# A graph network's counting groups with ten slots in two sets, their bounds loaded ahead, and the heads' additions on VectorE

## The reference, cut to what matters

```python
# first attention level, H = 8 heads, C = 768
h = (x @ W).reshape(n, H, C)
alpha_s = jnp.einsum('nhc,hc->nh', h, a_s)
alpha_d = jnp.einsum('nhc,hc->nh', h, a_d)
e = jax.nn.leaky_relu(alpha_s[src] + alpha_d[dst], NEG_SLOPE)
m = jax.ops.segment_max(e, dst, num_segments=n)
e = jnp.exp(e - m[dst])
denom = jax.ops.segment_sum(e, dst, num_segments=n)
alpha = e / (denom[dst] + EPS)
out = jax.ops.segment_sum(h[src] * alpha[:, :, None], dst, num_segments=n) + b
h = jax.nn.elu(out)          # and h @ W2 goes into the second level
```

## Time and profile before

| what | us |
|---|---|
| runs | 1856.82, 1858.04, 1856.78, median 1856.82 |
| the profiled execution, its own time | 1852.02 |
| its span, first to last instruction | 1849.9 |
| PE busy, mean granted clock | 1708.2, 0.971 |
| PE weight loads | 1387.4 |
| DVE busy | 1283.4 |
| ACT busy | 772.0 |
| POOL busy | 558.3 |

### The profile page before, as it was taken

How to read it: one execution, slowest core, us unless ns; L and a number is a source line. 1 busy time by engine, 2 the same in 40 slices (tenths; PEclk the granted TensorE clock), 3 DMA queues, 4 the chain that set the end, 5 groups by cost and what they waited for, 6 DMA issues and landing times. The chain is left out here.

```text
span 1849.9 us, 22198 instructions
## 1 busy us (share of the span) xinstructions
PE 1708.2 (92%) x7573; PEld 1387.4 (75%) x7582; DVE 1283.4 (69%) x2168; ACT 772.0 (42%) x1276; POOL 558.3 (30%) x319
## 2 busy tenths in 40 slices
PE   3779999999989999999999899999999994989998
PEld 1248888878867878777778777788787872878898
DVE  6654445544588877888789778887888428984437
ACT  4213332222345554455345545554455324534240
POOL 0012312212234533354335334434354213320003
PEclk9989999999999999999999999999999996989999
DMA  3015565495564546455555644566454412132123
GB/s 129 1 55 173 188 220 195 160 232 189 171 235 129 191 157 151 133 200 171 177 117 190 196 121 141 188 169 164 126 195 160 156 54 78 52 115 77 52 70 118
DMA packets 133808, 268.02 MB, mean 145 GB/s; under 512 B 23739, under 2 KB 83525, under 8 KB 121029
## 3 DMA queue, kind: packets, MB, share of 16 engines
q1 hardware_dynamic: 133700, 266.63, 45.6%
HBM read 206.21 MB, written 60.40 MB: 144 GB/s over the span
## 5 line engine op out<-in xcount | busy, mean ns | idle before, releaser
L466 POOL TENSOR_TENSOR w2l<-w2r,w2h 128x768 fp32r<-128x768 f32 x96 | 210.7, 2195 | 353.6 <-ACT w2h L587 353.6
L41 PE MATMUL bank<-ph,hc 128*128 128x512 f32 x768 | 300.9, 392 | 11.4 <-DVE mean L877 10.2
L42 PE MATMUL bank<-pl,hc 128*128 128x512 f32 x768 | 300.2, 391 | 0.0
L43 PE MATMUL bank<-ph,hc 128*128 128x512 f32 x768 | 300.1, 391 | 0.0
L753 DVE CUSTOM_DVE_ANT_0 junk<-bank,a_bc 128x512 bf16<-128x512 f32 (+1 forms) x256 | 129.9, 554 | 192.7 <-ACT st L527 176.8
L41 PE MATMUL bank<-hh,w2h 128*128 128x512 f32 x576 | 230.7, 400 | 21.8 <-DVE hl L886 18.3
L462 POOL TENSOR_TENSOR psum_rows<-psum_rows,pf 128x512 f32<-128x512 f32 x96 | 165.8, 1727 | 213.1 <-DVE pf L811 213.1
L41 PE MATMUL bank<-wh,xTh 128*128 128x512 f32 x570 | 224.0, 393 | 5.4 <-POOL wl L452 5.4
L43 PE MATMUL bank<-hh,w2l 128*128 128x512 f32 x576 | 226.5, 393 | 0.0
L42 PE MATMUL bank<-hl,w2h 128*128 128x512 f32 x576 | 226.1, 392 | 0.0
L42 PE MATMUL bank<-wl,xTh 128*128 128x512 f32 x570 | 222.6, 391 | 0.0
(11 more groups left out here) (245 smaller groups left out, 3081.3 us busy)
## 6 DMA issues: line engine op xcount, KB each, us to landing
hc<-h_scratch SPq DMA_DIRECT2D x96, 1024.0 KB, 4.9
h_scratch<-st SPq DMA_DIRECT2D x96, 512.0 KB, 3.0
w2r<-in_L_gnn_W SPq DMA_DIRECT2D x96, 384.0 KB, 4.9
wr<-in_L_gnn_W SPq DMA_DIRECT2D x12, 1536.0 KB, 8.5
gwr<-in_L_gnn_W SPq DMA_DIRECT2D x24, 384.0 KB, 3.3
row_bc<-logits_scratch SPq DMA_DIRECT2D x16, 512.0 KB, 10.5
expo_bc<-expo_scratch SPq DMA_DIRECT2D x16, 512.0 KB, 5.8
xr<-in_x SPq DMA_DIRECT2D x2, 1536.0 KB, 8.2
```

The lines of the kernel that those rows point to most:

```text
L41: nc.tensor.matmul(out, sh, mh, start=first, stop=False, skip_group_check=not grouped)
L42: nc.tensor.matmul(out, sh, ml, start=False, stop=False, skip_group_check=not grouped)
L43: return nc.tensor.matmul(out, sl, mh, start=False, stop=last, skip_group_check=not grouped)
L466: nc.gpsimd.tensor_tensor(w2l[:, g % 3, :], w2r[:, g % 3, :], w2h[:, g % 3, :].bitcast(F32), ALU.subtract).then_inc(w2_lo, 1)
```

## The change

In the counting stage: 32 tiles of `hot_low` are ACT's and 96 are DVE's. Tiles come in pairs. A window has eight fixed tiles (`FIRM`) written without a loop, and then a loop over at least one more pair; by the edges' order fifteen windows take ten tiles and one takes twelve, 162 in all. `hot_key` has two sets of ten slots, used in turn, so that DVE may work on window w as soon as window w-2 is finished. The first product of a window clears the bank itself. All 32 bounds are loaded to registers ahead: on PE before everything else of the stage, on DVE four behind each of the first eight `hot_low` operations. x is turned by float32 products with the identity in place of transposes, three pieces ahead of the windows; its low part comes from a product with the negative identity that leaves the rest in the bank (`lessen_x`), copied out by ACT.

In the heads: POOL's additions and subtractions are DVE's (but for six additions ahead of turn 0). `psum_rows` is split to `psum_h` (ACT) and `psum_l` (DVE), and `sum_weights` is two float32r products; DEN_EPS is added in the first addition; `inverse` is the reciprocal alone and reads the bank; the gather of the next turn waits for it. The exponents stand at the start of a turn, and the other steps in a new order, with ACT's and SP's to match.

```diff
-ACT_TILES = 40
-QT = 4
-EQ = ET // QT
+ACT_TILES = 32
+FIRM = 8
+SLOTS = FIRM + 2
+EP = ET // 2
...
-    hot_key = put("hot_key", 143360, [P, QT, NB * WD], BF16)
+    hot_key = [put("hot_key0", 143360, [P, SLOTS, NB * WD], BF16), put("hot_key1", 165888, [P, SLOTS, NB * WD], BF16)]
...
-            for i in range(1, NB):
-                sum_rows(0, i)
-            for u in range(U):
-                v, g = u + 1, u * FB
-                second_low(g)
-                for after, chunk in ((1, 1), (2, 2), (3, None), (4, None), (5, 3), (6, None), (7, 4)):
-                    if v < U:
-                        sum_rows(v, after)
-                    if chunk:
-                        second_low(g + chunk)
-                second_low(g + 5)
+            for i in range(2, NB):
+                pool.wait_ge(p_full, i + 1)
+                pool.wait_ge(p_sum, i - 1)
+                nc.gpsimd.tensor_tensor(psum_rows[:, :], psum_rows[:, :], pf[:, i % 2, :], ALU.add).then_inc(p_sum, 1)
...
+            ranges = []
             for j in range(ACT_TILES // TG, ET // TG):
...
+                if j == ACT_TILES // TG:
+                    dve.wait_ge(range_done, 9)
+                for w in range(2 * (j - ACT_TILES // TG), min(2 * (j - ACT_TILES // TG) + 2, NW)):
+                    ranges.append((dve.value_load(range_i[w:w + 1, 0:1], min_val=0, max_val=ET - SLOTS),
+                                   dve.value_load(range_i[w:w + 1, 1:2], min_val=FIRM // 2 + 1, max_val=EP)))
...
             for w in range(NW):
-                first = dve.value_load(range_i[w:w + 1, 0:1], min_val=0, max_val=EQ - 1)
-                quads = dve.value_load(range_i[w:w + 1, 1:2], min_val=1, max_val=EQ)
-                with dve.Fori(0, quads) as q:
...
+                first, pairs = ranges[w]
+                if w >= 2:
+                    dve.wait_ge(count_full, w - 1)
+                for j in range(FIRM):
+                    nc.vector.tensor_scalar(hot_key[w % 2][:, j, :], lane[:, :], keyT[:, 0, bass.ds(first + j, 1)], float(-NB * WD * w),
+                                            ALU.subtract, ALU.is_equal).then_inc(hot_ready[w], 1)
+                with dve.Fori(FIRM // 2, pairs) as q:
...
+            def sum_low(v):
+                dve.wait_ge(sum_hi, v + 1)
+                nc.vector.tensor_tensor(psum_l[:, :], psum_rows[:, :], psum_h[:, :].bitcast(F32), ALU.subtract).then_inc(sum_lo, 1)
...
-                nc.vector.tensor_scalar(rden[:, :], bank[:, :], DEN_EPS, None, ALU.add).then_inc(den_out, 1)
-                dve.wait_ge(den_out, v + 1)
-                nc.vector.reciprocal(rden[:, :], rden[:, :]).then_inc(rden_done, 1)
+                nc.vector.reciprocal(rden[:, :], bank[:, :]).then_inc(rden_done, 1)
...
-                    last = nc.tensor.transpose(x_bank(g)[:, j * P:(j + 1) * P], xr[:, 4 * half + j, f * P:(f + 1) * P], ident[:, :])
+                    last = nc.tensor.matmul(x_bank(g)[:, j * P:(j + 1) * P], xr[:, 4 * half + j, f * P:(f + 1) * P], ident[:, :],
+                                            start=(j == 0), stop=False, skip_group_check=True)
...
+            def lessen_x(g):
+
+                f, half = g % FB, g // FB
+                pe.wait_ge(x_hi, g + 1)
+                nc.tensor.matmul(x_bank(g)[:, :], neg_ident[:, :], xTh[:, f, half * HALF:(half + 1) * HALF],
+                                 start=False, stop=True, skip_group_check=True).then_inc(x_less, 1)
+
+            pe.wait_ge(range_done, 9)
+            ranges = [(pe.value_load(range_i[w:w + 1, 0:1], min_val=0, max_val=ET - SLOTS),
+                       pe.value_load(range_i[w:w + 1, 1:2], min_val=FIRM // 2 + 1, max_val=EP)) for w in range(NW)]
...
                 elif k == 0:
-                    pe.wait_ge(den_out, u + 1)
+                    pe.wait_ge(rden_done, u + 1)
                     pe.wait_ge(p_lo, (u + 1) * NB)
...
             def sum_weights(v, bank):
-                pe.wait_ge(p_sum, v * 7 + 7)
-                nc.tensor.matmul(bank[:, :], ones[:, :], psum_rows[:, :], start=True, stop=True).then_inc(den_full, 1)
+                pe.wait_ge(sum_lo, v + 1)
+                nc.tensor.matmul(bank[:, :], ones_r[:, :], psum_h[:, :], start=True, stop=False)
+                nc.tensor.matmul(bank[:, :], ones_r[:, :], psum_l[:, :], start=False, stop=True).then_inc(den_full, 1)
```

More of the change, by code:

```diff
@@ L212, in graph_and_heads @@
     rows = put("rows", 120832, [P, 4, HC], F32)
+    psum_h = put("psum_h", 120832, [P, HALF], F32R)
+    psum_l = put("psum_l", 122880, [P, HALF], F32R)
     e1 = put("e1", 126976, [P, 2, HALF], F32)
@@ L258, in graph_and_heads @@
     XG = 2 * FB
-    X_AFTER = {w: (w,) for w in range(XG)}
-    X_LOW_AFTER = {w + 1: (w,) for w in range(XG)}
+    X_BEFORE = 3
     BLOCK_AT = {(b // 2, 1 + 4 * (b % 2)): b for b in range(NB)}
@@ L513, in _ @@
             nc.scalar.copy(gcn_bias1[:, :], banks[4][:, 256 + 2 * FB:256 + 3 * FB]).then_inc(cols_done, 1)
+            for g in range(X_BEFORE):
+                x_high(g)
             for w in range(NW):
@@ L607, in leave, with sum_high @@
                     nc.scalar.copy(cols[:, f, :], banks[3 * i + f][:, :]).then_inc(cols_out, 1)
+            def sum_high(v):
+                act.wait_ge(p_sum, v * 7 + 7)
+                if v == 0:
+                    act.wait_ge(main_full, STEPS)
+                if v == H + 1:
+                    for i in range(4):
+                        act.wait_ge(rows_saved[i], 32)
+                nc.scalar.copy(psum_h[:, :], psum_rows[:, :]).then_inc(sum_hi, 1)
+            sum_high(0)
             for u in range(U):
@@ new lines, in _ @@
+                if w >= 2:
[4 more added lines that the diff above has]
+                with dve.Fori(FIRM // 2, pairs) as q:
+                    for j in range(2):
+                        dve.wait_ge(hot_free[w], q * 2 + (j + 1))
+                        nc.vector.tensor_scalar(hot_key[w % 2][:, FIRM + j, :], lane[:, :], keyT[:, 0, bass.ds(q * 2 + first + j, 1)], float(-NB * WD * w),
@@ L912, in _ @@
                 if more:
-                    weights(v, 2)
+                    if u == 0:
+                        dve.wait_ge(main_full, STEPS)
+                    weights(v, 0)
                 head_sum(g)
                 if more:
+                    weight_low(v, 0)
+                head_low(g)
+                if u == 0:
+                    exponents(w, top_junk[:, :])
+                if more:
+                    weights(v, 1)
+                    sum_rows(v, 1)
                     weight_low(v, 1)
-                head_low(g)
+                if u == 0:
+                    second_low(0)
+                    second_low(1)
+                second_low(g + 2)
                 average(g + 1)
@@ L946, in _ @@
                 if more:
+                    sum_rows(v, 5)
+                second_low(g + 4)
+                if more:
+                    weights(v, 6)
+                    weight_low(v, 6)
+                    sum_rows(v, 6)
+                average(g + 4)
+                if more:
                     weights(v, 7)
-                    weight_low(v, 6)
+                head_sum(g + 4)
+                if more:
                     weight_low(v, 7)
-                if w < U:
-                    exponents(w, top_junk[:, :])
-                average(g + 4)
-                head_sum(g + 4)
                 head_low(g + 4)
+                if more:
+                    sum_rows(v, 7)
+                    sum_low(v)
+                second_low(g + 5)
                 average(g + 5)
```

195 lines of the change are left out of this document (112 added, 83 removed).

## The result

The changed kernel takes 1781.96 us (median of four runs, 1778.77 to 1783.97), against 1856.8 before: a ratio of 0.9604, interval 0.9574 to 0.9633. It is faster by 75 us where 56 were forecast, and lies under the low end of the range (1784). The forecast's sum was made against the profiled execution; there the span goes from 1849.9 to 1779.8, 70.1 us less. The other 4.8 us are the distance of the profiled execution before to its own median; after, the two are the same (1781.86).

The account below looks back on a forecast made before the run. TensorE was taken to bound the heads, with 33 us idle; in counting, TensorE and VectorE wait for each other. Heads -39 and counting -17 sum to -56, taking the median from 1856.8 to 1800 us; range 1784 to 1820.

Parts of the forecast that it names:

- (h): Counting groups: 5.1 us with turn_x, 3.6 or 3.3 without, 4 for half-clock spells; with the later start, stage -17 us.
- (g): Counting stage's register loads: 32 at 0.61 us ahead make counting start at about 34 in place of 24.5, +9.5 us.
- (b): Heads: without GpSimd's work VectorE's operations fall to their minimum, so it takes on the additions at 49.2 us a head.
- Rival 2: Heads: VectorE's long operations are not GpSimd's doing and stay, VectorE becomes the bound; slower, halfway 1924 us; chance 0.03.
- (a): Heads: column sum as two float32r matmuls, 0.45 in place of 0.9 us; a head without waits from 58.0 to 57.6.
- (c): VectorE's order in a head: exponents (5.6 us) moved to its start clear the late chain to hl; no wait in normal heads.
- (d): End of a head: next gather waits for the reciprocal, 3.4 us to spare; no wait, 0.3 a head left for restarts.
- (e): Head 8: keeps its 24 transposes (3.4 us) and some wait for its row tiles, +4 us.
- (f): Head 0: the 7.6 us wait goes, but project(0) waits for w2l behind the exponents until about 563; 0 to +1 us.
- the stages that I took as unchanged: Main products (125.5 to 540.8) and everything behind 1450.3: instructions kept apart from one more VectorE addition, no change.
- the fourth: Rival 4, counting stage: relief better than granted, loads grouped cheaper and turn_x 0.6; 1788 us, chance 0.10.

Follow-up runs that it names:

- firm_two: The changed kernel with FIRM 2 in place of 8: two key tiles of a window fixed, the others through the loop of pairs; median 1814.4 us.
- turn_twice: The changed kernel with the four float32 products of each turn_x issued twice; median 1794.0 us.
- loads_inside: The changed kernel with a window's two register loads back at the head of that window on both engines; median 1781.8 us.
- three_places: The changed kernel with only windows 9 to 15's bounds loaded ahead, head 0's w2h copies and w2l subtractions earlier, head 8's row stores earlier; 1768.65 us.
- pool_busy: The changed kernel with thirteen additional GpSimd tensor-tensor operations per head, whose results nobody reads; 1885.1 us, ratio to before 1.0108.
- exponents_late: The changed kernel with the exponents of heads 3 and on back between the last sum_rows and mean(g+4), SyncE's saving moved with them; median 1788.9 us.
- best_two: three_places with head 0's w2h, w2l and first hh, hl still earlier, and saving of exponents and row_bc load behind head 8's row stores; 1755.33 us.

## Why the prediction was right and wrong

The direction was right, and most mechanisms; the time was not, and the failed step is **(h), the size of a counting group**. It said 5.1 us for a window with turn_x, 3.6 and 3.3 without; they are 3.41, 2.5 and 2.2. Two terms were too dear.

- The keys and the loop: eight matmuls at a pitch of 0.26 and 1.1 for a loop of one pair, 3.2 in all. Measured 2.17 for all ten, a pitch of 0.217. The 0.26 is not in the quads that it was read from: their 1.07 holds the last matmul's own 0.39, so the starts are 0.227 apart. The 1.1 is the price of a turn behind another one, with a jump back and reused slots (the second pair of window 5 costs just that); the only turn of the other fifteen windows has neither. firm_two shows it from the other side: with two slots to reuse in three or four further turns, each of these costs 1.03, and the stage is 31 us longer. 1.03 x 16 windows = 16.5 us of the miss.
- turn_x: 1.5, from the weight loads' durations. The weight loads of turn_x overlap the matmuls and each other (in the trace after eight of 0.19 each take 0.97 together), so a duration isn't a pitch: 0.86 in the trace, 0.89 by turn_twice. Nine windows, 5.8 us of the miss.
- The 4 us for half-clock spells: none came. Before, the stage had a clock of 0.92 and spells such as twelve matmuls in 4.49 us; after, 1.00. What set them off before isn't settled: firm_two waits 0.4 before three of four pairs, and its clock is 1.00 too.

16.5 + 5.8 + 4 + 0.5 for the earlier start (zero product at 33.5) make 27; less the 0.3 by which the second pair costs more than my 0.8 and the 1.0 between the last count and the first main product, this is the 25 by which the stage was missed. My own lower bound of -26 for the stage had turn_x at 0.61 but kept the 1.1 and the 0.26.

**(g)** was right: hot_low operations of VectorE stand 2.5 us apart, one for each four loads, and the first key matmul stands at 33.8 (forecast about 34). Two of them in the trace after:

```profile
26.24 1.23 DVE L738 TENSOR_TENSOR hot_low<-lane,keyT 128x1024 bf16<-128x1024 f16 x1 [1.29 <-issue]
28.75 4.63 DVE L738 TENSOR_TENSOR hot_low<-lane,keyT 128x1024 bf16<-128x1024 f16 x4 [1.29 <-issue]
```

The thirty-two loads on VectorE's sequencer start 0.65 apart on average, as against 0.62 to 0.64 for the two of a pair before (0.90 for the first). With this the floor of about 600 ns in the Trainium skill's page DMA: Bandwidth & Descriptors (Latency and other measured facts) agrees; a saving from loading several together does not show. loads_inside and three_places give the worth of their place: 9 us at the start.

**(b)** was right, and is most likely the heart of the heads' gain: of the 37 us the column sum gives 5.5 and the place of the exponents 5 at most; how the rest divides between the relief and the other steps of the new order is not measured. `pl` at 0.692, w2l 0.954, the added additions 0.685, DVE busy 46.4 us per head (forecast 49.2). pool_busy brings the long operations back by GpSimd's work alone. The rule of the Trainium skill's GPSIMD Engine Reference (Key points), that GpSimd contends with VectorE's instructions of two SBUF inputs, agrees with `pl` and `mean` in both traces, but not every such instruction is longer in pool_busy (last section). Rival 2, slower, had 0.03. Its reason, long operations that aren't GpSimd's doing, is refuted; what it feared isn't far: with GpSimd about as busy as before (21.7 us in a head against 25.2) VectorE becomes the bound, and the kernel takes 1.1% longer than before.

**(a)** was right to 0.01: 57.61, and 58.00 with the float32 sum. **(c)** was right in that no head waits, but its reason was too narrow: exponents_late shows that the new place of the exponents is worth some 5 us of the 37 at most, and that nine of thirteen heads have no wait without it. **(d)** held, without the 0.3 a head for restarts. **(e)** was too small: head 8 costs 11.4 over the others, not 4, through row tiles whose stores stood behind row_bc and the chunks of later heads, as best_two shows with 3.3. **(f)** named the very wait, project(0) for w2l behind the exponents, and put its end at 563 of the old trace, 22 us behind the column sum; it came at 522.7, 23 us behind it. What I left out was what follows: hc for gather 4 is 2.5 late, and behind the two waits ten and seven matmuls start 0.43 apart in place of 0.227 at a clock of 0.50 and 0.52, 3.6 us. With the 1 us by which project(0) is later these make up the 7.2 us.

So the heads gave 29.5 where 39 were forecast, and the counting 42 where 17 were. That the profiled sum (-70) came out 14 under mine is the 25 of (h) less 9.5 of the heads (7.4 of (e) and 6.2 of (f), against them the 4.2 for restarts in (d) that weren't needed) and 1.5 of the stages that I took as unchanged.

Of the rivals the fourth named the right terms (loads, turn_x), but only one of them moved.

## What to carry to other kernels

The cost of a loop's turn, read where two engines hand each other slots, belongs to the hand-over and the jump back; ask, before pricing a version that hands out more slots and turns once, what each engine needs alone. Price pipelined matmuls by the distance of their starts, never by the duration of a matmul, of a merged row or of a weight load. Register loads belong where the engine behind them has a backlog: here behind each large one-hot operation and in windows where TensorE has other work, which is 8 us better than all of them ahead. And when a change moves an order for the steady turn, follow the first turn and the odd one (here heads 0 and 8) on every queue, SyncE's too: they held the 17 us by which best_two's heads are shorter than those of after.

## What the runs showed of the hardware that was not expected

GpSimd's operations lengthen VectorE's to very different degrees: in pool_busy `pl` takes 1616 ns on average in heads 1 to 14 (692 without), `hl` 1204 (693), w2l 1133 (955), psum_rows 861 (685), while `e` (678) and `pf` (692), which read two SBUF tiles as well, stay at their minimum. By their place in the order these run just before GpSimd is started, but no run here separates that from their kind. A float32 product of 128 columns costs 0.22 us (two instructions, 0.107 apart), no more than a bfloat16 matmul of 512 columns at 0.217. A first loop of one turn behind fixed matmuls added nothing that the trace shows.
